# Rounds 4 to 15 of the attention part: U in three reduced-precision passes, scores in two halves, softmax in pairs

## The reference

```
xn = layernorm(x)
q, k, v = xn @ Wq + bq, xn @ Wk + bk, xn @ Wv + bv        # 4 heads of 256
scores = (q*cos . k*cos + q*sin . k*sin) / 16             # per token, 4 x 4 heads
out = softmax(scores) @ v, heads swapped with tokens, reshaped
s = out @ Wo + bo
gates = sinkhorn((xn @ rw + rb) / temp, 3); the two largest of 8 experts
g = silu(xn + sum over 2 experts of gate * ((relu(xn @ wg) * (xn @ wp)) @ wo))
x + s * g
```

## Time and profile before

| | |
|---|---|
| median of 3 runs | 1589.72 us (1585.95 to 1590.04) |
| profiled execution, its own time | 1588.45 us |
| its span, first to last instruction | 1586.7 us |
| busy in the span: TensorE, VectorE, ScalarE, GpSimd | 1528.8, 1017.2, 731.9, 795.3 us |
| rounds 4 to 14 | from 1000.3 to 1524.5 us |
| round 15 and the end | from 1524.5 to 1586.7 us |

### The profile page before, as it was taken

The page is one execution under the profiler, slowest core; times in us unless marked ns, Lnnn a source line. Parts: engine busy times, 40 slices in busy tenths (PEclk is TensorE's granted clock), DMA queues, the critical chain, the costliest instruction groups (busy, mean ns, idle before and its releaser), DMA issues.

```text
span 1586.7 us, 31308 instructions
## 1 busy us (share of the span) xinstructions
PE 1528.8 (96%) x10868; PEld 1141.1 (72%) x10868; DVE 1017.2 (64%) x2015; ACT 731.9 (46%) x1205; POOL 795.3 (50%) x945
## 2 busy tenths in 40 slices
PE   5999799989999999999999999999999999999997
PEld 2546666668888888888888888776666776666773
DVE  7567989954444444444444444678888888888777
ACT  5766334413333333333333333556456565555552
POOL 4648589823434443444344433262584664753456
PEclk9999799989999999999999999999999999999999
DMA  9988842265233241323111321346555566445464
GB/s 326 394 326 324 308 175 83 73 225 182 71 121 118 71 135 58 116 74 135 57 54 58 110 108 44 103 153 203 174 170 179 200 194 220 163 157 168 153 206 147
DMA packets 173298, 251.14 MB, mean 158 GB/s; under 512 B 15336, under 2 KB 122656, under 8 KB 173024
## 3 DMA queue, kind: packets, MB, share of 16 engines
q1 hardware_dynamic: 158528, 211.48, 39.0%
q0 software_dynamic: 12960, 35.41, 6.7%
q10 hardware_dynamic: 1664, 2.26, 0.4%
HBM read 149.58 MB, written 99.50 MB: 157 GB/s over the span
## 4 chain that ended last, share of the span: by engine, by line
PE 90%; DVE 5%; DMA 1%; issue 1%; ACT 1%; SPq 1%; ACTq 0%; DVEq 0%
PE ps L1151 23%; PE ps L1086 22%; PE ps L1097 13%; PE ps L1170 12%; PE ps L1033 7%; PE ps L1160 4%; PE ps L1054 2%; PE ps L1133 2%; PE ps L1002 2%; PE ps L930 1%; PE ps L986 1%; PE ps L920 1%; DVE UN L1236 1%; DMA WR<-w_d 1%; ACT WM L823 0%
## 5 line engine op out<-in xcount | busy, mean ns | idle before, releaser
L1151 PE MATMUL ps<-WR,FR 128*128 x1620 | 404.8, 399 | 2.7 <-DMA WR<-w_d 2.7
L1151 PEld LDWEIGHTS ps<-WR,FR 128*128 128x128 f32 x1620 | 295.6, 189 | 58.0 <-issue 3.0
L1663 DVE TENSOR_TENSOR AUX<-AUX,ps 128x512 f32<-128x512 f32 x135 | 92.9, 688 | 338.4 <-ACT AUX L862 338.4
L655 POOL DMA_INDIRECT y_d<-AUX x135 | 133.6, 990 | 348.7 <-DVE AUX L1652 348.4
L823 ACT ACTIVATE WM<-ps,bcs,trig 128x512 f32<-128x512 f32 x256 | 254.4, 1018 | 90.7 <-PE ps L1086 82.9
L1599 DVE TENSOR_SCALAR WM<-ps,vec,trig 128x512 f32<-128x512 f32 x256 | 245.2, 994 | 63.1 <-ACT WM L823 62.6
L1097 PE MATMUL ps<-WM,XTJ 128*128 128x512 f32 x512 | 237.1, 600 | 0.0
L862 ACT ACTIVATE AUX<-ps 128x512 f32<-128x512 f32 x135 | 81.0, 600 | 315.1 <-PE ps L1151 289.8
L1086 PE MATMUL ps<-XH,WH 128*128 128x512 f32 x512 | 206.5, 403 | 4.9 <-issue 4.0
L1170 PE MATMUL ps<-WR,ABR 128*128 x540 | 207.1, 418 | 0.0
L1086 PE MATMUL ps<-XL,WH 128*128 128x512 f32 x512 | 201.3, 393 | 0.6 <-issue 0.6
(11 more groups left out here) (239 smaller groups left out, 2255.0 us busy)
## 6 DMA issues: line engine op xcount, KB each, us to landing
US<-u_d SPq DMA_DIRECT2D x63, 512.0 KB, 4.7
u_d<-UN SPq DMA_DIRECT2D x120, 256.0 KB, 2.0
WR<-w_d SPq DMA_DIRECT2D x96, 256.0 KB
AUX<-y_d SPq DMA_DIRECT2D x32, 512.0 KB, 5.8
WM<-in_L_attn_x_dram SPq DMA_DIRECT2D x16, 512.0 KB, 9.6
xn_d<-WM SPq DMA_DIRECT2D x32, 256.0 KB, 7.4
w_d<-USR SPq DMA_DIRECT2D x16, 512.0 KB, 4.6
AUX<-xn_d SPq DMA_DIRECT2D x16, 512.0 KB, 6.1
```

Of the source, the lines that this page charges most:

```text
L655: e.indirect_dma_start(y_d, bass.IndirectOffsetOnAxis(toks[:, n:n + 1], 0), YS[n % 4], None).then_inc(s_y[n % 4], 16)
L1151: mm = e.matmul(b[:, :], x, WR[:, bass.ds(off[m] + (2048 * z + 1024 * a + 512 * k), 512)], start=(k == 0 and x is xh and z == 0), stop=(k ...
L1663: e.tensor_tensor(HS[:, m % 2, :], GR[:, :], mP[m % 2][:, :], ALU.mult).then_inc(s_h, 1)
```

## The change

In the late rounds:

- U is made of three float32r products, as the projections are: `XHJ` and `XLJ` (high and low part of the tokens, in U's order) against `MH` and `ML`. ScalarE makes XHJ and XLJ with four copies (`xj`) at the end of the round before; GpSimd's `xtj` is gone there.
- `MH` and `ML` are made during the expert stage, in sixteen pieces through DRAM: ScalarE's queue loads a piece of M, VectorE splits it (`split_m`), ScalarE's queue stores it; SyncE loads both parts at the end of the stage.
- The projections run in two sets, even chunks `P0` and odd chunks `P1`, each followed by U chunks. The scores are accumulated in two halves (`half_scores`), one behind P0 and four U chunks, one at the end of the round. So q and k need half the room (`QH`), and banks 4 and 5 hold the scores over the round. The projections' ring is given by a table.
- The softmax, and the spreading of its weights, take two quarters at once (`soft_a2`, `soft_b2`, `spread2`).
- The silu of the round before stands behind P1 (chunk 15) and no longer behind chunk 18, that of a hosted early round behind chunk 23 and no longer between two exponentials. `early` stands behind chunk 9. In round 15 the silus, loads and `ahead` move forward.

`lone` returns False for every chunk, so VectorE still does all sine halves.

```diff
+        P0, P1 = tuple(range(0, 16, 2)), tuple(range(1, 16, 2))
+        def order(q):
+            if q < QE:
+                return tuple(range(24))
+            if q < NQ - 1:
+                return P0 + (16, 17, 18, 19) + P1 + (20, 21, 22, 23)
+            return P0 + tuple(range(16, 24)) + P1
+        BANKS = {c: (0, 1, 6, 7, 2, 0, 1, 2)[i] for i, c in enumerate(P0)}
+        BANKS.update({c: (1, 2, 6, 7, 0, 1, 2, 0)[i] for i, c in enumerate(P1)})
+        def bank(q, c):
...
+            if q < NQ - 1:
+                return (0, 1, 2, 0, 1, 2, 0, 1)[c - 16]
+            return (c - 16) % 3
+        def mixes(q):
+            if q < QE:
+                return {18: 0, 20: 1, 22: 2, 23: 3}
+            return {19: 0, 20: 1, 23: 2, 24: 3} if q == NQ - 1 else {19: 0, 24: 1, 21: 2, 23: 3}
+        def turns(q):
+            return {17: 0, 20: 1} if q < QE else {20: 0, 22: 1}
...
+            def xj(q):
+                e.wait_ge(s_xtd, 2 * q + 2)
+                e.wait_ge(s_ch, 24 * q if q == QE else at(q - 1, 23))
+                if q == QE:
+                    e.wait_ge(s_dn, NM)
+                for k in range(2):
+                    for v, w in ((XHJ, XH), (XLJ, XL)):
+                        ins = e.activation(v[:, k, :, :],
+                                           w[:, k, :].bitcast(F32).rearrange("p (r j) -> p j r", j=4), ACT.Copy)
+                    ins.then_inc(s_xtj, 1)
...
+                for xx, w in ((XHJ, MH), (XHJ, ML), (XLJ, MH)):
+                    mm = e.matmul(b[:, :], xx[:, k, j, :], w[:, k, cols],
+                                  start=(k == 0 and xx is XHJ and w is MH), stop=(k == 1 and xx is XLJ))
...
+            def half_scores(q, h):
+                e.wait_ge(s_ca, at(q, 14 + h))
+                e.wait_ge(s_cd, rotated_by[q, 14 + h])
+                if h == 0:
+                    e.wait_ge(s_sm1, 4 * q)
...
+            def split_m(i):
+                e.wait_ge(s_mr, 16 * (i + 1))
+                ch(e.tensor_copy(UNR[:, 1, :], UN[:, 0, :]))
+                e.tensor_tensor(UNR[:, 2, :], UN[:, 0, :], UNR[:, 1, :].bitcast(F32), ALU.subtract).then_inc(s_msp, 1)
...
+                            if c == 16:
+                                spread2(n)
+                                biased(n)
+                            elif c == 17:
+                                biased(n + 1)
+                            if c in mixes(q):
+                                mixed(n + mixes(q)[c])
+                                if mixes(q)[c] == 1:
+                                    spread2(n + 2)
+                                    biased(n + 2)
+                            if c == (23 if q == NQ - 1 else 20):
+                                biased(n + 3)
...
-                        if q - 1 in host and c == 8:
+                        if q - 1 in host and c == 9:
                             early(host[q - 1])
```

More of the change, by code:

```diff
@@ L86, in program @@
         XL = sb("XL", [128, 2, 512], F32R)
+        with nc.sbuf_tensor("XHJ", [128, 2, 4, 128], F32R) as XHJ:
+            pass
         XTJ = sb("XTJ", [128, 2, 4, 128])
+        with nc.sbuf_tensor("UNR", [128, 3, 512], F32R) as UNR:
+            pass
         UN = sb("UN", [128, 3, 512])
@@ L298, in us, with piece @@
             return XB[:, :, :] if n == 4 * NQ - 1 else US[:, n % 3, :, :]
+        def piece(i):
+            return slice(512 * i, 512 * i + 512)
+        raw_at, split_at, kept_at = ({7 * i + d: i for i in range(16)} for d in (2, 4, 6))
         def blk(ap, q):
@@ L428, in load_c, with load_x @@
                     e.dma_start(xx[h:128:4], rows(xf, q)[h]).then_inc(sl, 16)
+            def load_x():
+                e.wait_ge(s_ch, at(NQ - 1, 17))
+                for h in range(H):
+                    e.dma_start(cs(NQ - 1)[3][h:128:4], rows(xf, NQ - 1)[h]).then_inc(s_xe, 16)
             def load_e(k):
@@ L817, in segment @@
                 for q in range(q0, q1):
-                    for c in range(24):
-                        e.wait_ge(s_ch, 24 * q + c + 1)
-                        b = ps[bank(24 * q + c)][:, :]
+                    for c in steps(q):
+                        if c == 24:
+                            if q == NQ - 1:
+                                silu(q)
+                            continue
+                        e.wait_ge(s_ch, at(q, c))
+                        b = ps[bank(q, c)][:, :]
                         if c < 16:
                             x, i = c // 8, c % 8
-                            e.activation(rotated(2 * x, i), b,
+                            if lone(q, c):
+                                e.activation(rotated(q, 2 * x + 1, i), b, ACT.Identity, bias=bcs[:, x, 1, i:i + 1],
+                                             scale=trig[:, 1, i:i + 1])
+                            e.activation(rotated(q, 2 * x, i), b,
                                          ACT.Identity, bias=bcs[:, x, 0, i:i + 1],
@@ L1080, in segment @@
                     e.wait_ge(s_xtd, 2 * q + 2)
-                    for c in range(24):
-                        b = ring(24 * q + c)
+                    for c in steps(q):
+                        if c == 24:
+                            half_scores(q, 0)
+                            if c in mixes(q):
+                                mix(4 * q - 4 + mixes(q)[c])
+                            continue
+                        b = ring(q, c)
                         if c < 16:
@@ L1113, in segment @@
                         scores(4 * q + i)
-                        if q == NQ - 1 and i >= 2:
-                            mix(4 * q + i - 2)
                         place(lists.get((q, 24 + i), ()))
                 if q1 == NQ:
-                    mix(4 * NQ - 2)
-                    mix(4 * NQ - 1)
+                    e.wait_ge(s_ca, at(NQ - 1, 15))
+                    e.wait_ge(s_cd, rotated_by[NQ - 1, 15])
+                    for i in range(4):
+                        mix(4 * NQ - 4 + i)
             e.wait_ge(s_wsp, 4)
@@ L1623, in segment @@
                             soft_b(n - 1)
-                        if q == NQ - 1 and i:
-                            spread(n - 1)
-                            if i == 3:
-                                mixed(n - 3)
                         if (q, 24 + i) in firsts:
@@ L1630, in segment @@
                     soft_b(4 * q + 3)
-                if q1 == NQ:
-                    spread(4 * NQ - 1)
-                    for i in range(1, 4):
-                        mixed(4 * NQ - 4 + i)
             segment(0, QE)
```

278 lines of the change are left out of this document (207 added, 71 removed).

## The result

| | before | after |
|---|---|---|
| median (14 runs each) | 1589.88 us (1585.57 to 1595.08) | 1575.96 us (1571.87 to 1584.71) |
| ratio | | 0.9914, 95% from 0.9898 to 0.9929 |
| profiled execution: own time, span | 1588.45, 1586.7 | 1574.38, 1572.6 |
| rounds 4 to 14 | 1000.3 to 1524.5: 524.2 | 996.5 to 1509.4: 512.9 |
| round 15 and the end | 62.2 | 63.2 |

The kernel is 14 us faster, where 30 were forecast. So 10.3 us were gained in the late rounds of this profile.

What follows compares the result with a forecast made beforehand. TensorE was taken to bound the late rounds, VectorE next. U's -43.4 and -5 for old gaps, less new waits and small terms, summed to -29.6: 1560 us predicted, forecast case 1550 to 1573 (0.59), range 1544 to 1580.

Steps and rivals of the forecast that it cites:

- the gaps of before: TensorE's late-round idle gaps, read as mixes waiting for VectorE, 4.9 us; counted as gone: -5.
- The scores have as many products as before: Scores in two halves on TensorE: no added cost by count, 3.84 us for each half.
- -43.4: U in three passes, rounds 4 to 15: a chunk goes from 1.81 to 1.36 us at the projections' beat.
- The new waits: Waits between engines that the change adds in the late rounds, taken as 17 us together.
- the first mix: End of P0 to the first mix: TensorE waits for VectorE's `biased`, 0.4 a round, +4.8 (0 to 14).
- P1's ring: P1's chunks wait for banks held by VectorE's sine halves, 0.2 a round, +2.2 (0 to 10).
- `early`: Two VectorE operations in P1 of rounds 6, 8, 10, 12 delay a sine half: 1.8 each, +7.4 (5.6 to 11.6).
- the second transpose: At U chunks 20 to 23 TensorE waits for the tokens' low part: 0.15 a round, +1.8 (0 to 3.6).
- (+1): End of round: ScalarE's four strided `xj` copies, 0.8 each, delay P0; 1 us for all rounds (0 to 12).
- Round 15 and the end: Last stretch, 62.2 us before, to take 59.3; beyond savings counted elsewhere, +1.1 (-1 to 3).
- Rivals 1 to 4: Smaller waits, 1546 (0.12); VectorE slowed, 1584 (0.10); slower three passes, 1570 (0.07); late copies, 1607 (0.06, 0.08 with VectorE's late blocks).
- rival 5: All gains given back by unseen waits, a late load of US or store of UN: 1588, chance 0.04.

Runs made afterwards that it cites:

- e8_silu_in_u: e6_quiet_scores with the hosted round's silu moved on ScalarE to behind the second U copy of the next round, between P0 and P1: 1559.14 us.
- second profile: Profile of e0_guard, the changed kernel with two register waits rewritten as asserted values: 1574.63 us.
- e0_guard: The changed kernel with the expert stage's two waits on loaded register values rewritten as asserted values: 1574.63 us.
- e2_loads_later: The changed kernel with loads for hosted endings and round 15's ending issued behind the fourth U store: 1569.86 us.
- e4_early_silu: The changed kernel with `early` moved out of P1 behind the first mix, and round 14's silu moved behind round 15's: 1569.79 us.
- e3_more_traffic: The changed kernel with four more 512 KB DRAM transfers ahead of the U stores of rounds 6, 8, 10, 12 and 13: 1587.5 us, one run.
- e6_quiet_scores: The changed kernel with late-round loads issued behind the fourth U store, beside P1, `early` between the last mixes and round 14's silu moved: 1564.2 us.
- float32 pair: U in two float32 matmuls, same TensorE program: on the changed kernel 1596.33 us, on e8_silu_in_u 1586.66 us.
- clean pair: e8_silu_in_u, 1559.14 us, against the same kernel with U of rounds 4 to 15 in float32 again, 1586.66 us.

## Why the prediction was wrong

The late rounds by what TensorE does, each stretch from its start to the start of the next (us; an idle piece ahead of a stretch counts with the one before it, so "scores" has the wait for round 15's softmax too):

| | before | after | e8_silu_in_u |
|---|---|---|---|
| U | 174.3 | 141.2 | 141.9 |
| scores | 98.1 | 111.4 | 99.5 |
| projections | 263.6 | 275.1 | 267.8 |
| transposes | 10.2 | 7.8 | 7.8 |
| mixes | 40.2 | 40.5 | 39.5 |
| rounds 4 to 15 | 586.4 | 576.1 | 556.5 |

**The step that failed** is in two sentences: "I count them as gone: **-5**", on the gaps of before, and "The scores have as many products as before [...] and cost nothing by count: 3.84 for each half". The count was right (3.88 each where undisturbed). But the gaps of the earlier trace rows that stand at L1033, 2.9 us, do not lie "where a mix waits for VectorE late in a round", as the prediction reads them. They lie inside the scores, each ends 2.2 to 2.6 us after the start of a block of instructions, and the forecast moved half of the scores to the part of the round where the DMA engines are full.

By the earlier trace rows the DMA share is 0.53 over rounds 4 to 14, an average that hides this: in the 2 us before the start of those blocks it is 0.77 to 1.05 already in before. In the profile of after it is 0.8 to 1.1 in the 8 us before the first half scores of rounds 6 to 15 and 0.00 to 0.49 over P1. The pieces came to 10.5 us, the matmuls behind them ran at the lower clock, and all half scores together with what follows them to the next start took 111.4 us against 98.2 where nothing disturbs them; in the second profile 102.3. So the scores came out 13.3 us dearer than before where they were to be 2.9 cheaper, 16 us off, the largest single error.

What shows the cause are runs of one and the same TensorE program with other traffic beside it. With the traffic left where the change put it, or more of it (e0_guard, e2_loads_later, e4_early_silu, e3_more_traffic), 15 of the 16 first half scores of rounds 6, 8, 10 and 12 have a piece of over 0.25 us (0.35 to 5.99); with the traffic moved (e6_quiet_scores, e8_silu_in_u) 1 of 8 has one (0.51). In the float32 pair it is 4.5 us against none. `early` was moved in e4_early_silu as well, and its pieces stayed. Added to the old order, the traffic brings 1.6 to 3.5 us into each of the five rounds chosen. And in twelve profiles, before and after included, each of the 41 idle pieces of over 0.25 us in projections or scores that no engine explains ends 2.2 to 2.9 us after a 16 KB block began on queue 8. Full engines alone don't do it, as rounds 7, 9, 11 and 14 of e2_loads_later show: I take it that TensorE has to come to the end of the block that it holds just then, which no view of the profile shows. The one piece of e8_silu_in_u stands apart, with a DMA share of 0.06 in the 2 us before its block.

The Trainium skill, Runtime: NRT & Kernel Launch, section Instruction fetch mechanics, says that each engine's sequencer fetches instructions in blocks of 16 KiB, 256 instructions, through a DMA queue of its own, and calls the cost "mostly hidden". The traces agree on the size of a block and, in calm rounds, on the cost; with the DMA engines full, a piece is up to 6.0 us. The block's start is what is late: 9 of the 41 begin only after TensorE has gone idle, up to 3.8 us after, and these packets take 0.9 to 1.5 us, no more than others. Open is what holds the start back. A comparison with scores of fewer instructions wasn't tried.

**U: right mechanism, size off by 10 us.** -43.4 was forecast; U took 174.3 us before and 141.2 after, -33.1. In the clean pair, where both have the new order, it is -27.6. A chunk behind another chunk takes 1.36, as forecast, but three in eight stand behind a mix or a transpose and take 1.49 to 1.57, and the mean is 141.2 / 96 = 1.47, with the waits ahead of mixes in it (1.7 in the list, 2.0 with those too short for it). And the 1.81 of before held such a switch as well; a float32 chunk behind another takes 1.71. I compared a price with the switch with one without.

**The new waits** were summed at 17 us and came to about 7: the first mix 1.1 (+4.8 forecast), P1's ring 0.5 (+2.2; 1.7 in e0_guard), `early` 5.3, as P1 takes 49.4 in its four rounds against 4 x 11.02 (+7.4), and the second transpose nothing: the transposes take 7.8 us in all, before 10.2 (+1.8). Round 4's P0 takes 0.8 more than the others (+0.5). `biased` averages 1.52 us in after. The one of 1.21 that the prediction puts between two pieces of GpSimd's work runs beside one of them, from 1266.52 on, whose record is 1.79 us long. `xj` took more than taken, 4.6 us for the four copies, yet cost TensorE next to nothing (+1): P0 takes 11.01 to 11.05 from round 5 on, as a P1 without waits does. From 1000 to 1525 us of after,

```profile
L906 ACT ACTIVATE ABR<-XL 128x512 fp32r<-128x512 f32 x23 | 26.3, 1142 | 0.0
L906 ACT ACTIVATE XHJ<-XH 128x512 fp32r<-128x512 f32 x22 | 25.5, 1159 | 0.0
```

1.15 each, near the strided end of the range. The Trainium skill, ScalarE: Activation LUTs, section What ACT_TABLE_LOAD costs, has 186 + 0.833 N ns with no term for the stride, which would be 0.61, an estimate that these copies don't bear out. The prediction's 0.71 for the rotation is worked out for one pointer operand, and the code gives it two, the scale and the bias, so its comparison with the 0.78 measured says nothing. The experts cost nothing, as forecast (652.4 against 652.6).

**Round 15 and the end**: 63.2 in place of 59.3. The second softmax pair's weights wait until the first two mixes have read `AT`, and TensorE, idle for 4.97 us before, does the mixes at the lower clock (0.50 granted from 1560.7 to 1569.2):

```profile
1551.82 3.95 PE L1186 MATMUL ps<-WM 128*64 128x64 f32 x128 [1.81 <-DVE WM L1812]
1560.74 1.10 PE L1209 MATMUL ps<-US,AT 128*32 128x256 f32 x8 [4.97 <-issue]
1561.57 1.13 PE L1211 MATMUL ps<-BR,AT 128*32 128x256 f32 x8
```

In sum: the late rounds gained 10.3 us in the profile of after where 29.6 were forecast. Of the 19.3 missing, U is 10.3 and the scores 16; the other terms came out 7 better than forecast. The 1559 of e8_silu_in_u stands where the forecast did by luck: U brought 32.4 there, 11 less than forecast, and all the rest cost 2.5 in place of 13.8, in a kernel whose loads, silu and `early` stand elsewhere than in the one forecast. Rivals 1 to 4 priced waits between engines; rival 5 spoke of late transfers, but of data alone.

## What to carry to other kernels

An idle piece "issue" in the middle of one run of matmuls, with no releaser, is not slack that a reordering recovers: look in the DMA queues for an instruction block just ahead of its end. Before a dense burst of small instructions is moved, read the DMA share by windows of a few microseconds at its old and its new place, not the stage's mean. The cure is in the order of the transfers: here the same bytes, issued some 15 to 20 us later into idle DMA time, with `early` out of P1, brought 10 us, and 15 with one silu moved, against 14 for the change itself. And when an edit shifts an engine's program, expect such pieces to move to other places: compare runs with the same program on that engine.

## What was not expected of the hardware

- An idle TensorE in the middle of 128 ready matmuls, for up to 5.99 us, behind one late 16 KB block; a 4.02 us piece cost its round 5.3 us in all, the granted clock being 0.58 in the 3.6 us behind it.
- ScalarE copies 512 elements in 0.60 us contiguously, and in 1.15 where it reads them with a stride of four.
- Whether a round can have such a piece goes by the place in the program, whether it has one by the traffic: with one TensorE program all of them inside half scores stood in even rounds, with another in 7, 9, 11 and 14, though the DMA share before the half scores was 0.8 to 1.1 in both kinds of round.
- Two profiled executions took the same time, 1574.38 and 1574.63 us, with late parts of 576.1 and 565.7: in one the first expert matmul stands at 343.7, in the other at 354.5. A stretch has to be compared with the same stretch.
